# Turning two probability tiles one step earlier in a fused macaron (FFN, attention, FFN) kernel

## The reference

```python
q = (x @ Wq).reshape(B, T, H, D).transpose(0, 2, 1, 3)     # H = 32 heads, D = 128
k = (x @ Wk).reshape(B, T, G, D).transpose(0, 2, 1, 3)     # G = 8 groups, 4 heads each
v = (x @ Wv).reshape(B, T, G, D).transpose(0, 2, 1, 3)
q = _apply_rope(q, cos, sin)
k = _apply_rope(k, cos, sin)
scores = jnp.einsum('bgrtd,bgsd->bgrts', qg, k) * D ** (-0.5)
scores = jnp.where(causal, scores, -jnp.inf)
probs = jax.nn.softmax(scores, axis=-1)
out = jnp.einsum('bgrts,bgsd->bgrtd', probs, v)
return out @ Wo + bo
```

## Time and profile before

| | |
|---|---|
| median of 3 runs | 1498.8 us (1497.66 to 1503.31) |
| the profiled execution, its own time | 1500.57 us |
| its span | 1498.3 us |
| PE busy | 1393.6 us, 93% |
| DVE busy | 1229.7 us, 82% |
| ACT busy | 875.4 us, 58% |
| POOL busy | 531.1 us, 35% |
| transposes `pTf<-phl` | 512, median 2.9 us from issue to landing |

### The profile page before, as it was taken

How to read it: one execution, slowest core, us unless ns; L and a number is a source line. 1 busy time by engine, 2 the same in 40 slices (tenths; PEclk the granted TensorE clock), 3 DMA queues, 4 the chain that set the end, 5 groups by cost and what they waited for, 6 DMA issues and landing times.

```text
span 1498.3 us, 26151 instructions
## 1 busy us (share of the span) xinstructions
PE 1393.6 (93%) x8832; PEld 795.5 (53%) x8962; DVE 1229.7 (82%) x3107; ACT 875.4 (58%) x2166; POOL 531.1 (35%) x440
## 2 busy tenths in 40 slices
PE   5578999998999999999999998999999999999965
PEld 4344554554555655555555654555555555555533
DVE  6777979998988977989787987889778888888744
ACT  3367676666665665556655665565655656555623
POOL 0375655655542232233422322323323333323102
PEclk9799999999999999999999999999999999999988
DMA  6158767768765555555554644565555565655413
GB/s 228 42 148 193 190 161 168 192 168 190 165 148 108 135 129 107 126 127 120 124 138 106 141 121 98 120 136 117 130 130 138 137 137 125 141 118 124 100 31 112
DMA packets 409555, 201.12 MB, mean 134 GB/s; under 512 B 352176, under 2 KB 353392, under 8 KB 409424
## 3 DMA queue, kind: packets, MB, share of 16 engines
q1 hardware_dynamic: 407312, 195.25, 56.0%
q10 hardware_dynamic: 2112, 4.19, 0.8%
HBM read 90.30 MB, written 25.17 MB: 77 GB/s over the span
## 4 chain that ended last, share of the span: by engine, by line
PE 67%; DVE 16%; ACT 7%; issue 4%; POOL 3%; DMA 1%; SPq 1%; DVEq 0%; ACTq 0%
PE PJ L1096 16%; PE PJ L1097 15%; PE PJ L1095 14%; PE PV L1095 3%; PE PV L1097 3%; PE PV L1096 3%; PE SC L1254 3%; PE SC L1255 3%; PE SC L1256 3%; DVE phl L910 3%; ACT p L584 3%; POOL t L453 3%; DVE p L899 2%; DVE t L872 2%; DVE t L871 1%
## 5 line engine op out<-in xcount | busy, mean ns | idle before, releaser
L453 POOL TENSOR_TENSOR t<-t 128x512 f32<-128x512 f32 x160 | 203.3, 1271 | 714.0 <-DVE t L872 713.8
L584 ACT ACTIVATE p<-p,mn 128x512 f32<-128x512 f32 (+3 forms) x512 | 281.0, 550 | 185.6 <-DVE mn L899 185.5
L910 DVE SCALAR_TENSOR_TENSOR phl<-p,ri,phl 128x512 f16<-128x512 f32 (+3 forms) x512 | 303.8, 616 | 0.0
L593 ACT ACTIVATE phl<-p,ri 128x512 f16<-128x512 f32 (+3 forms) x512 | 244.6, 550 | 18.9 <-DVE ri L1006 16.9
L1095 PE MATMUL PJ<-XTh,wsp 128*128 128x512 f16 x640 | 243.4, 380 | 3.7 <-DVE t L872 2.3
L1096 PE MATMUL PJ<-XTl,wsp 128*128 128x512 f16 x640 | 243.1, 380 | 0.0
L1097 PE MATMUL PJ<-XTh,wsp 128*128 128x512 f16 x640 | 243.1, 380 | 0.0
L899 DVE CUSTOM_DVE_ANT_0 p<-SC,maskw 128x512 f32<-128x512 f32 (+3 forms) x512 | 219.7, 485 | 2.9 <-PE SC L1256 0.6
L1096 PE MATMUL PJ<-wosp,oTf 128*128 128x512 f16 x512 | 196.0, 383 | 10.9 <-DVE raw L751 5.7
L1097 PE MATMUL PJ<-wosp,oTl 128*128 128x512 bf16 x492 | 188.3, 383 | 0.0
L456 POOL TENSOR_TENSOR qTl<-t,qTh 128x512 f16<-128x512 f32 x128 | 148.3, 1159 | 95.0 <-ACT qTh L566 95.0
(11 more groups left out here) (187 smaller groups left out, 2573.7 us busy)
## 6 DMA issues: line engine op xcount, KB each, us to landing
wsp<-kept SPq DMA_DIRECT2D x144, 256.0 KB, 2.9
wosp<-kept SPq DMA_DIRECT2D x96, 256.0 KB, 3.3
raw<-in_wqkv SPq DMA_DIRECT2D x48, 256.0 KB, 4.8
kept<-wsp SPq DMA_DIRECT2D x48, 256.0 KB, 2.3
raw<-in_wo SPq DMA_DIRECT2D x32, 256.0 KB, 5.0
pTf<-phl SPq DMA_TRANSPOSE x512, 2.9
kept<-wosp SPq DMA_DIRECT2D x32, 256.0 KB, 2.9
X<-in_x ACTq DMA_DIRECT2D x4, 1024.0 KB, 11.1
```

The lines of the kernel that those rows point to most:

```text
L453: nc.gpsimd.tensor_tensor(t1[:, j, :], t1[:, j, :], t2[:, j, :], ALU.add).then_inc(rope_sum, 1)
L584: ins = nc.scalar.activation(pt, pt, ACT.Exp, bias=mn[:, par, i:i + 1], scale=-1.0, accum_out=rs[:, par, i:i + 1])
L593: nc.scalar.activation(phl[:, par, POFF[i]:POFF[i] + w], p[:, par, SOFF[i]:SOFF[i] + w], ACT.Copy, scale=ri[:, par, i:i + 1]).then_inc(a_p ...
L910: nc.vector.scalar_tensor_tensor(out=phl[:, par, POFF[i] + w:POFF[i] + 2 * w], in0=p[:, par, SOFF[i]:SOFF[i] + w], scalar=ri[:, par, i:i + 1],
```

## The change

DVE's and SP's streams are written in another order; no instruction is added or removed. The low halves of the two widest tiles (`k` = 0 and 1) of step `s` were made behind the minima of step `s + 1`, ahead of that step's reciprocal. Now they are made in step `s` itself, behind its rope and `out_lo`. The two narrow ones (`k` = 2 and 3) stay in step `s + 1`, where they now are alone. SP's transposes follow: two of step `s` at the end of step `s`, two behind the refills of step `s + 1`.

```diff
-            def turn(s):
+            def turn(s, ks):
                 par = s % 2
-                for k, i in enumerate(ORDER):
+                for k in ks:
+                    i = ORDER[k]
                     w = (i + 1) * P
                     sp.wait_ge(d_pl, 4 * s + k + 1)
...
                 if s:
-                    turn(s - 1)
-            turn(NS - 1)
+                    turn(s - 1, (2, 3))
+                turn(s, (0, 1))
+            turn(NS - 1, (2, 3))
...
                 minima(s)
                 if s:
-                    p_lo(s - 1, 0)
-                    p_lo(s - 1, 1)
+                    p_lo(s - 1, 2)
                 dve.wait_ge(a_exp, 3 * s + 3)
                 nc.vector.reciprocal(ri0[:, :], rs[:, par, :]).then_inc(d_rec, 1)
                 if s:
-                    p_lo(s - 1, 2)
+                    p_lo(s - 1, 3)
                 dve.wait_ge(d_rec, s + 1)
                 nc.vector.tensor_scalar_mul(ri[:, par, :], ri0[:, :], PSCALE).then_inc(d_norm, 1)
-                if s:
-                    p_lo(s - 1, 3)
                 for kind, m, idx, _ in queries_of(n, h):
                     rope(kind, m, idx)
                 if s >= 2:
                     out_lo(s - 2)
+                p_lo(s, 0)
+                p_lo(s, 1)
                 for stage, k, bb, i in side(DVE_A, DVE_B, s):
...
-            for k in range(TB):
-                p_lo(NS - 1, k)
+            p_lo(NS - 1, 2)
+            p_lo(NS - 1, 3)
             out_lo(NS - 2)
```

## The result

The changed kernel takes **1538.1 us** (median of 4 runs, 1536.7 to 1541.0), the kernel before 1501.05 (4 runs): a ratio of 1.0248, 95% interval 1.0225 to 1.0271. The direction was forecast, the size was not: +37 us where the sum said +10.

The account below looks back on a forecast made before the run. PE was taken to set the time after the first batch, with DVE becoming as full. +6 us in the middle, +2 last, +5 first and -3 returned gave +10 on 1500.6, 1510.6, stated as 1510; range 1488 to 1538.

Parts of the forecast that it names:

- The failed step: Added to DVE's need in every step: waits left when DVE and PE are equally loaded, 0.15 us between 0 and 0.56.
- the reading by the weight loads' share: Rejected reading of the whole kernel: DVE binds at 85% and each us gained counts in full, 199 us, some 1700 in all.
- (a): Ahead of the reciprocal: the wide tiles cost nothing there; once gone, 1.1 us a step turn idle, about 140 in all.
- (c): Behind `out_lo`: the two wide tiles cost their full 1.20 us a step, and their input is already there.
- (b): Behind the reciprocal: rope 0.24 us earlier; the scaling that frees `p_hi` 0.16 later, hidden because ACT starts 2.2 us behind it.
- (d): Behind `out_lo`: the first wide tile waits for POOL's L453, 0.5 us in every step, bounds nothing and 1.4.
- (e): Steps behind a key rope: ACT's exps come late and delay the reciprocal, 0.1 us a step, bounds 0 and 0.2.
- The first batch: First 32 steps: need 10.40 plus 0.5 for POOL's weight splitting gives 10.9, plus 0.15 of waits, +5 us.
- (f): Transposes: the last lands earlier, PE's waits for `pTf` go to near nothing; 3 of 4.1 us come back at the end.
- The waits come back: Rival: DVE's idle time takes all the moved work and PE's transpose waits return; faster, 1481 to 1490 us, chance 0.20.
- No change: Rival: the middle stays within DVE's 1.6 us idle, first batch's gain and loss cancel; 1499 us, chance 0.30.
- POOL gets ahead of the second wide tile: Rival: behind `out_lo`, POOL also delays the 384 wide tile in a third of the steps; 38 us more, 1548, chance 0.12.

Follow-up runs that it names:

- experiment 4: The changed kernel with the two wide tiles put behind the last work of their step instead of directly behind `out_lo`: 1606.5 us, ratio 1.0706.
- the last of 8: Changed order, narrow tiles in the gap ahead of the reciprocal, the previous step's residual addition behind `out_lo`: 1544.5 us, ratio 1.0279.
- n2_before: The kernel before with POOL's rotary sum and its low half both narrowed from 512 to 32 columns: 1476.1 us, ratio 0.983.
- n_before: The kernel before with only POOL's rotary sum narrowed from 512 to 32 columns: 1477.9 us, ratio 0.9839.
- g_fill: The changed kernel with the residual addition and the 256 wide tile also drawn into the gap ahead of the reciprocal: 1498.7 us, ratio 0.9976.
- n2_after: The changed kernel with POOL's rotary sum and its low half both narrowed from 512 to 32 columns: 1478.5 us, ratio 0.9845.
- pad_one: The kernel before with the low half of the attention output computed once more in each step: 1522.7 us, ratio 1.0139.
- g_pad: g_fill with the low half of the attention output computed twice: 1506.3 us, ratio 1.0026.
- f_spkeep: e_fill with SP's stores of the split weights issued behind the two narrow transposes: 1502.0 us, ratio 0.9994.
- e_fill: The changed kernel with the last step's residual addition drawn into the gap ahead of the reciprocal: 1503.2 us, ratio 1.0014.
- n2_pad: n2_before with the low half of the attention output computed three times per step: 1497.9 us, ratio 0.9967.
- e_one: The change made for the 512 wide tile only, the 384 wide one staying ahead of the reciprocal: 1536.0 us, ratio 1.0238.
- pad_two: The kernel before with the low half of the attention output computed twice more in each step: 1558.6 us, ratio 1.0376.
- n_after: The changed kernel with only POOL's rotary sum narrowed from 512 to 32 columns: 1517.1 us, ratio 1.0096.
- e_four: The changed kernel with all four tiles made and turned in their own step: 1676.3 us, ratio 1.1173.
- experiment 7: SP's stores of split weights issued behind the transposes: 1536.7 us in the changed kernel, 1502.2 in the kernel before, 1502.0 in e_fill.
- experiment 8: Versions of the changed kernel with the gap ahead of the reciprocal filled further; the one with the copy is g_pad, 1506.3 us.

## Why the prediction was right in direction and wrong in size

**The failed step is the one that takes 0.15 us of its "between 0 and 0.56"**, for two engines of nearly equal load. The path was right: the moved tiles, the gap and the contention made DVE as full as PE. DVE's need was forecast at 10.67 us in the middle and measured at 10.73. But the step came out 11.10 long, 0.38 above the need: 0.18 of waits for the values' high halves, 0.06 for PE, 0.02 for other high halves, 0.12 of small gaps. The term of 0.15 thus measured 0.38. Held against PE's own 10.55, the step is 0.55 longer where I had 0.27.

The middle batches lost 22.5 us where 6 were forecast. Of the 26 us between the 36 measured and the 10 forecast these are 16, and the first batch has 7; 2.3 are the later start, which is scatter.

Need and step from step 32 to 96, for the kernels in which no missed input sets the step (those of experiment 4 and the last of 8 are off it, by PE's waits shown there):

```
kernel                      need us   step us
n2_before                      9.07     10.69
n_before                       9.12     10.69
before                         9.28     10.75
g_fill                         9.91     10.69
n2_after                       9.95     10.66
pad_one                       10.03     10.93
g_pad                         10.20     10.73
f_spkeep                      10.23     10.70
e_fill                        10.23     10.76
n2_pad                        10.40     10.83
e_one                         10.52     11.13
pad_two                       10.69     11.25
after                         10.73     11.10
n_after                       10.75     11.01
e_four                        11.90     12.13
```

(f_spkeep and e_fill have the same order in these batches; their 0.06 us shows how well such a step repeats. The other two kernels of experiment 7, left out here, stand within 0.01 us of after and of before.)

There is a floor of 10.69 that is PE's: a need of 9.07 and one of 9.95 give the same step within 0.03 us. So the reading by the weight loads' share, in which DVE binds and each us that it gains counts in full, is wrong here, as the prediction held. (It also took only half of the page's rule: the Trainium skill's "Perfetto Trace Analysis", Identifying the Most-Contended Engine, names the matmuls' work as a share of peak, MFU, beside the weight loads' share.) Up to a need of about 10.2 most kernels stay on the floor, at 10.5 to 10.7 they are 0.3 to 0.6 above it, and in the one kernel far beyond, the step is the need plus 0.2. So the step begins to grow before the two loads are equal.

The likely reason is that the steps differ, and that I compared averages over a batch. In after DVE's work alone goes from 7.8 to 11.1 us in a step and PE's from 8.4 to 11.3 (13.2 once a batch), and the two do not rise and fall together: DVE's need is the larger in 30 of the 64 steps (its step runs from first minimum to first minimum, PE's from first score to first score). If every step took the larger of the two, the mean would be 10.73 us in before and 11.34 in after, where the steps took 10.75 and 11.10. The rise is there, but this sum does not give its size: for e_fill it says 11.12, and the step took 10.76. The engines make up part of their lateness in a light step, and which part is not shown.

One kernel lies off the curve, pad_one, and what sets it apart from n2_pad, which has more need and a shorter step, stays open. Contention in single steps and latency are both possible; by n_after 0.9 us less of the latter was worth 0.09 us a step.

**The gap (a)** held: 149.7 us of waits for "about 140". **(c)** held: the 384 wide tile takes 0.605, and the wide tiles never wait for their high halves for more than 0.2 us. **(b)** held in its cost and not in its reason: the later scaling is not hidden, since ACT waits for it 106 times (24.6 us in all, and 16.9 in 20 times before). No tile on DVE had to wait for that.

**The contention (d)** held: for "0.75 + 0.5" the 512 wide tile took 1272 ns in the first batch, 1254 in the middle and 1237 in the last. That it spares the second tile held too; the rival that hung on it fell. What I had not looked for is the same contention on the 128 wide tile (517 in place of 322 ns). It adds to the busy time and is taken off the gap.

**The key ropes (e)** were not measured by themselves; the need hit by 0.06 us says that no more than that is missing in the sum of (a) to (e), where errors may also have cancelled.

**The first batch** was forecast at 10.9 + 0.15 and came out at 11.03 + 0.23: 12 us for 5. The estimate of 0.5 for POOL's weight splitting was 0.13 short.

**What comes back (f)** failed by its words and held in its sum. PE's waits for `pTf` did not go to near nothing, they went from 27.2 to 20.5 us. SP issues the narrow transposes behind its stores; moving those halved the waits and gave no time that the intervals show: waits for DVE came in their place, as the prediction says of the first batch. The 3 us at the end came (2.7).

**The last batch** had 9.80 + 0.15 forecast: need 9.87, step 10.09, +2 us as summed.

**The rivals.** "The waits come back" wanted a need that grows by under 1.2 in the later batches and under 0.8 in the first; it grew by 1.45 and by 1.01. "No change" wanted the middle to stay within DVE's idle time, and by its letter it did: the need of 10.73 is below the old step of 10.75. The step grew all the same, which is the failed step once more. The filled version (g_fill), with growth under 0.7, is what "no change" looks like. "POOL gets ahead of the second wide tile" fell with the 605 ns of that tile, though its 1548 is nearer to the measured time than my 1510.

## What to carry to other kernels

Before work is moved out of a place where its engine has to wait anyway, count that place as part of the engine's load: the work leaves and the wait stays. Here 1.2 us of moved work and 0.5 us of contention added 1.45 us of need, and putting 0.7 us of other work into the empty place gave nearly all of the time back.

When two engines serve the same steps, do not take the larger of two average loads as the time. Compared step by step the rise shows, though such a sum says too much (11.34 for 11.10 us). Here the time began to rise when the second engine's average stood about 0.5 us of 10.7 below the first's, and at equality it was 0.3 to 0.6 us a step above either.

Put a filler where its engine is idle and no other engine waits for its result: the same residual addition won 35 us when it was moved into the gap, and cost 46 us when it was moved on from there, some five microseconds later in the step.

## What the runs showed of the hardware

Contention between DVE and POOL depends on where DVE's operands lie. In after, DVE's instructions of 512 columns that lie beside a POOL instruction for over 0.2 us, against those beside none: `p_lo`, with both tensors in SBUF, 1255 ns on the mean of 126, against 750 (2); `out_lo`, one of them in PSUM, 692 (124) against 687 (4); the residual addition, from PSUM too, 683 (75) against 682 (48). The statistics of L705, one tensor in SBUF, 691 (17) against 685 (31); but a normalisation that also reads one tensor in SBUF, L747, 1329 (4) against 538 (13).

The one that asks second waits until shortly before the end of the other's instruction. In the step shown above the two wide tiles lose 1.78 - 1.28 = 0.50 us, so the first begins at 604.08, 0.21 ahead of POOL's end at 604.29; the narrow one loses 0.49 and begins 0.17 ahead of it. It holds the other way too, in part: POOL's low half of the query (L458), which in after mostly comes while a wide tile still has 0.34 us to run, takes 1.36 us on the mean of 125, and the key's, which comes beside none, 1.16 (32). The Trainium skill's "SBUF — State Buffer" (SBUF: two separate sides) has the pair of ports that both share as an exclusive lock, held by the first for its whole instruction, and taken by DVE in a two-port mode or with two SBUF inputs. The trace agrees but for the last 0.2 us. L747, with one tensor in SBUF, could be slow beside POOL by such a two-port mode, which no run here shows directly.

The wait can be used: work that reads PSUM fills it. In experiment 8 a copy of 0.69 us took 0.47 us off the 512 wide tile behind it (1216 ns in g_fill, 742 with the copy).
